# A small-batch gated feed-forward with gathered LoRA weights on one core: section three's weights queued after A of tile 1, both A gathered ahead of both B, splits reordered

## The reference

```python
def lora_add(base, inp, A, B):            # A: (16, 16, ·), B: (16, ·, 16)
    Ab, Bb = A[0][lora_indices], B[0][lora_indices]      # one adapter per sequence
    t = einsum('bri,bni->bnr', Ab, inp)
    return base + einsum('bor,bnr->bno', Bb, t) * 0.5
gate = lora_add(x @ W_gate.T, x, A_gate, B_gate)         # F = 1376 columns
up   = lora_add(x @ W_up.T,   x, A_up,   B_up)
x = x + lora_add((silu(gate) * up) @ W_down.T, silu(gate) * up, A_down, B_down)
x = x + einsum('bct,bcd->bdt', x, weights[condition])    # a 32x32 mix per sequence
```

## Time and profile before

| | |
|---|---|
| median of 3 runs | 449.8 us (449.45 to 450.18) |
| the profiled execution | 449.22 us, of which the span is 447.4 us |
| PE busy | 439.1 us (98% of the span) |
| DVE, ACT, POOL busy | 335.8 (75%), 212.5 (47%), 170.3 us (38%) |
| moved by DMA | 81.12 MB, mean 181 GB/s |

### The profile page before, as it was taken

The page is one execution under the profiler, slowest core; times in us unless marked ns, Lnnn a source line. Parts: engine busy times, 40 slices in busy tenths (PEclk is TensorE's granted clock), DMA queues, the critical chain, the costliest instruction groups (busy, mean ns, idle before and its releaser), DMA issues.

```text
span 447.4 us, 7255 instructions
## 1 busy us (share of the span) xinstructions
PE 439.1 (98%) x2477; PEld 394.7 (88%) x2477; DVE 335.8 (75%) x625; ACT 212.5 (47%) x397; POOL 170.3 (38%) x156
## 2 busy tenths in 40 slices
PE   7989999999999999999999999999999999999997
PEld 5868888888888888888888888999999999999996
DVE  6858989888866867867857858977767766776665
ACT  6736345456444444444543444844444454444541
POOL 2711322130111221121121452675666766666630
PEclk9989999999999999999999999999999999999999
DMA  8965664448476565565565599847667666656631
GB/s 240 379 209 159 167 174 134 111 163 199 120 197 158 146 180 149 159 172 146 158 171 145 144 283 347 241 136 194 210 186 209 208 197 179 175 174 191 195 100 47
DMA packets 99987, 81.12 MB, mean 181 GB/s; under 512 B 50960, under 2 KB 83344, under 8 KB 99952
## 3 DMA queue, kind: packets, MB, share of 16 engines
q1 hardware_dynamic: 88512, 47.15, 37.9%
q0 software_dynamic: 11008, 33.30, 24.8%
q10 hardware_dynamic: 432, 0.22, 0.2%
HBM read 65.18 MB, written 15.47 MB: 180 GB/s over the span
## 4 chain that ended last, share of the span: by engine, by line
PE 93%; DMA 2%; POOL 2%; issue 1%; DVE 1%; ACT 0%; SPq 0%; POOLq 0%
PE bank L1393 28%; PE bank L1271 9%; PE bank L1272 9%; PE bank L1270 9%; PE bank L1225 7%; PE bank L1226 7%; PE bank L1227 7%; PE bank L1292 5%; PE bank L1293 4%; PE bank L1423 2%; POOL a_raw L455 2%; PE bank L1403 2%; DMA a_raw<-in_a_gu_rows,rows 1%; DMA gu_landing<-in_w_gate 1%; PE bank L1408 1%
## 5 line engine op out<-in xcount | busy, mean ns | idle before, releaser
L455 POOL DMA_INDIRECT b_raw<-in_b_rows,rows x48 | 51.9, 1082 | 189.8 <-DVE b_gu L809 188.4
L1393 PE MATMUL bank<-wd,actT_hi 128*128 128x288 f32 (+1 forms) x636 | 110.1, 295 | 0.1
L1393 PEld LDWEIGHTS bank<-wd,actT_hi 128*128 128x128 f32 (+1 forms) x636 | 93.8, 188 | 2.1 <-issue 0.9
L455 POOL DMA_INDIRECT a_dn_raw<-in_a_dn_rows,rows x64 | 77.7, 1214 | 19.5 <-issue 19.5
L809 DVE SCALAR_TENSOR_TENSOR b_gu<-b_raw,low_rows,b_gu 128x1024 fp32r<-128x1024 f32 (+1 forms) x48 | 55.6, 1158 | 24.2 <-ACT b_gu L515 20.4
L1393 PE MATMUL bank<-wd,actT_lo 128*128 128x288 f32 (+1 forms) x318 | 68.2, 296 | 0.7 <-issue 0.7
L1393 PEld LDWEIGHTS bank<-wd,actT_lo 128*128 128x128 f32 (+1 forms) x318 | 51.0, 188 | 0.4 <-issue 0.4
L515 ACT ACTIVATE b_gu<-b_raw 128x1024 fp32r<-128x1024 f32 (+1 forms) x48 | 46.2, 963 | 9.6 <-DMA b_raw<-in_b_rows,rows 7.8
L605 ACT ACTIVATE act<-bank 128x512 f32<-128x512 f32 (+1 forms) x48 | 26.2, 547 | 44.0 <-PE bank L1293 43.9
L916 DVE TENSOR_TENSOR act<-act,bank 128x512 f32<-128x512 f32 (+1 forms) x48 | 29.9, 623 | 9.2 <-PE bank L1293 7.6
L1292 PE MATMUL bank<-b_gu,tT_hi 128*128 128x512 f32 (+1 forms) x96 | 35.6, 371 | 0.3 <-DVE tT_lo L805 0.3
(11 more groups left out here) (180 smaller groups left out, 1009.7 us busy)
## 6 DMA issues: line engine op xcount, KB each, us to landing
actT_raw<-actT_dram SPq DMA_DIRECT2D x16, 640.0 KB
actT_dram<-staging SPq DMA_DIRECT2D x64, 128.0 KB
x_sb<-in_x SPq DMA_DIRECT2D x16, 256.0 KB
xT_raw<-in_xT SPq DMA_DIRECT2D x15, 256.0 KB
out<-out_sb SPq DMA_DIRECT2D x15, 256.0 KB
a_raw<-in_a_gu_rows SPq DMA_DIRECT2D x56, 64.0 KB
actT_dram<-staging SPq DMA_DIRECT2D x32, 88.0 KB
wd_raw<-in_w_down SPq DMA_DIRECT2D x10, 256.0 KB, 5.8
```

The source lines that it names most:

```text
L455: return pool.indirect_dma_start(dst, None, src, bass.IndirectOffsetOnAxis(ap=rows[:, tile, col:col + 1], axis=0))
L1393: last = pe.matmul(ps_down[e][half][:, 0:HALF], a[e][0:n, c, :], wd[0:n, c, part, at:at + HALF], start=(c == 0 and i == 0), stop=(c == NC ...
```

## The change

The weights of section three (16 to 23) are queued by SP only when all four gathers of A of tile 1 have landed. POOL starts at another signal: x of tile 1 landed, instead of x of tile 0 split. It then gathers A of both tiles and after them B of both. ACT's and DVE's lists follow: A of tile 1 is split ahead of B of tile 0, and section three's pieces are split later, two of them between t of tile 0 and t of tile 1, two more behind the gating of unit 1 (on ACT behind its silu) instead of ahead of t.

```diff
--- before.py
+++ after.py
@@ -415,7 +415,9 @@
             sp.dma_start(xT_raw[0][:, 2 * P:KH * P], xT[0:P, 2 * P:KH * P]).then_inc(xT_landed[0], 16)
             load_gate_up(2, 2 * KH)
             load_xT(0, 1)
-            load_gate_up(2 * KH, GU_PIECES)
+            load_gate_up(2 * KH, 4 * KH)
+            sp.wait_ge(a_first_landed[1], 16 * TILE_SEQS)
+            load_gate_up(4 * KH, GU_PIECES)
             pair(0, first=True)
             pair(1)
             pair(2)
@@ -490,10 +492,10 @@
                 gather(mix_raw[m % 2][:, :], mix_rows, m, 2 * TILE_SEQS + 2).then_inc(mix_landed[m % 2], 16)
 
             pool.wait_ge(rows_ready, 1)
-            pool.wait_ge(xT_ready[0], 1)
+            pool.wait_ge(xT_landed[1], 16)
             gather_first_a(0)
+            gather_first_a(1)
             gather_b(0, 0, 0)
-            gather_first_a(1)
             gather_b(0, 0, 1)
             for pr in range(PAIRS):
                 pair(pr)
@@ -687,17 +689,16 @@
             split_x(0, 1)
             split_weights(2 * KH, 4 * KH)
             split_a(0, 0)
-            split_weights(4 * KH, 4 * KH + 2)
+            split_a(0, 1)
             split_b(0, 0, 0)
-            split_weights(4 * KH + 2, 5 * KH)
-            split_a(0, 1)
             split_t(0, 0)
             split_b(0, 0, 1)
+            split_weights(4 * KH, 4 * KH + 2)
+            split_t(0, 1)
             silu(0, 0)
             split_b(0, 1, 0)
-            split_t(0, 1)
             silu(0, 1)
-            split_weights(5 * KH, 6 * KH)
+            split_weights(4 * KH + 2, 6 * KH)
             split_b(0, 1, 1)
             split_a(1, 0)
             silu(0, 2)
@@ -1052,19 +1053,19 @@
             split_x(0, 1)
             split_weights(2 * KH, 4 * KH)
             split_a(0, 0)
-            split_weights(4 * KH, 4 * KH + 2)
+            split_a(0, 1)
             ve.wait_ge(low_landed, 16)
             split_b(0, 0, 0)
-            split_weights(4 * KH + 2, 5 * KH)
-            split_a(0, 1)
             mask_t(0, 0)
             split_t(0, 0)
+            split_b(0, 0, 1)
+            split_weights(4 * KH, 4 * KH + 2)
             mask_t(0, 1)
-            split_b(0, 0, 1)
             split_t(0, 1)
             gate(0, 0)
             split_b(0, 1, 0)
             gate(0, 1)
+            split_weights(4 * KH + 2, 5 * KH)
             turn(0, 0)
             turn(0, 1)
             split_weights(5 * KH, 6 * KH)
```

## The result

| | before | changed |
|---|---|---|
| median | 449.8 us (449.45 to 450.45, 5 runs) | 452.63 us (451.84 to 453.83, 5 runs) |
| ratio | | 1.0072, 95% interval 1.0049 to 1.0096 |
| profiled execution, span | 449.22, 447.4 us | 453.83, 452.0 us |

The account below looks back on a forecast made before the run. PE was taken as the bound, with no slack after unit 4's start. L + 10.85 gives 36.75; plus 0.6 for the next gather, less the old 35.78, 1.57 us later: 449.8 + 1.6 = 451.4 us, range 449.6 to 453.3.

Parts of the forecast that it names:

- POOL's start and order: POOL's first gather at 11.3 us instead of 8.05; B of tile 0, ninth instead of fifth, starts at 22.0.
- Landing of A: Last gather of A of tile 1 lands at 23.9 us, `t_alone(1)` starts without a stall: 1.6 us gained on PE.
- L: Landing of B of section one for tile 0: 25.9 us, against 20.27 before; bounds 24.1 to 28.3.
- From L to unit 4: Chain of splits, masks and `lora(0,2)` from L to the start of unit 4: 10.85 us, so 36.75.
- The next gather: B of section two for tile 0, gathered once B of section one is split: 5.9 us to land, adding 0.6.
- rival (b): Clock falls again after PE's waits before `lora(0,0)` and `lora(0,2)`; if unit 4 runs low too, 453.1 us; chance 0.15.
- The rule of the Trainium skill: DMA engines alternate between queues with work, so the 0.6 us for B of section two would fall away: 450.8.
- Rival (a): The gathers run fast and the kernel is faster or the same, 449.0 us at L = 24.1; chance 0.23.
- Hidden parts: Two splits moved behind unit 1's gating cost nothing, cover 0.1 us; SP's loads of A of pair 1 end by 39.8.

Follow-up runs that it names:

- the control: The changed kernel once more, without an edit, beside the kernel before on the same chip: 453.24 us, where the kernel before had 449.58.
- the controls: The kernel before and the changed kernel, each run once more without an edit: 449.83 and 453.24 us.

## Why the prediction was right, and where it was off

Direction and range held, the range narrowly for the control (453.24 of 453.3); the size was too small by 1.2 us (1.6 forecast, 2.8 measured, 3.4 between the controls). The mechanism was the forecast one; one term of its sum, the next gather, was far too small.

- **POOL's start and order**: 11.3 forecast, 11.40 measured; B of section one starts at 22.0 and 22.40. Right.
- **Landing of A**: 23.9 and 23.5; no wait ahead of `t_alone(1)`. Right: the goal of the change was reached, 1.6 us of stall removed. The 64 KB gather took 2.4 us on quiet DMA (21.15 to 23.5), less than my 3.1.
- **L**: 25.9 and 26.1. Right. `lora(0,0)`: 29.75 and 29.94, PE idle 3.1 us.
- **From L to unit 4**: 10.85 forecast. In the four profiles in which ACT doesn't wait for B of section two it was 11.1 (three times) and 11.4. Right within 0.5.
- **The next gather**: here the sum failed. I took 5.9 us for B of section two and 0.6 us for its lateness. Beside the held weights it took 7.2, 7.1, 6.9, 7.6 and 7.5 us (five profiles); behind weights that wait for it 4.3 to 4.5 (three). Unit 4 then starts 3.5 us after its landing, 4.1 to 4.3 if the clock is low. In the changed kernel's profile that makes 2.4 us instead of 0.6 (0.7 of it is the low clock in `lora(0,2)`, see rival (b)), in its control 1.7. The 5.9 came from the gather at 45.52, of which the prediction says that DMA was full. The share was 0.98 and 0.89, but little was moved, against 392, 421 and 373 GB/s beside the gather in the changed kernel. In the kernel before:

```profile
46.00:48.00 2.00, 2.00 (x11) 1.65 (x10) 2.00 (x2) 0.03 (x1) 1.21 (x2) 1.00 0.98 168
48.00:50.00 2.00, 2.00 (x11) 1.71 (x10) 1.67 (x4) 1.09 (x2) 1.17 (x1) 1.00 0.89 301
```

- **The 4.64 us of the profile** add up: L + 11.1 is 37.2 instead of 35.78, 1.4 us; the next gather 2.4; unit 4 at the low clock 0.85.
- **The rule of the Trainium skill** ("DMA: Bandwidth & Descriptors", "Queues, rings and completion order") was taken to make this term nothing. The page says that each engine takes turns, not that a turn costs nothing: with an even share of the 367 GB/s of the earlier trace rows, an estimate, 512 KB would take 1.4 us more than the 4.3 to 4.5 without a backlog. The runs bear neither out: it took 2.8 us more beside the backlog. Nor does an even share fit the 7.6 us for 352 KB in the kernel with old start and no hold.
- **Rival (b)**, a second low clock, came true in the changed kernel's first profile and not in its control. By the mean clocks it isn't the usual case: 4 of the 11 executions of the changed kernel have 0.992, as much low clock as two spells of 3.6 us, and the other seven 0.995 or 0.996; the median execution, 452.63, has 0.995. It cost 0.7 us in `lora(0,2)` (37.91 to 39.57 instead of 0.95 us) and 0.85 in unit 4 (7.34 instead of 6.49), 1.6 for 3.4 us at the low level, against the 1.7 of the prediction; the Trainium skill's relation ("TensorE: Matmul & The Clock Gate", "Terms"), half the throttled time, agrees.
- **Rival (a)**, fast gathers, fell: POOL needed 11.0 us for eight, L was 26.1.
- **Hidden parts**: SP's loads of A of pair 1 ended at 38.4 and delayed nothing; the two splits moved behind unit 1's gating cost at most 0.1 us (unit 4 to unit 5 took 6.4 at full clock).

The cause in short: holding the weights until A of tile 1 has landed moves the backlog from that gather to the next one on the chain, B of section two. It is paid there, on top of B of section one that comes later by order and start. Undoing start or hold alone doesn't mend it (453.43, 453.67), undoing start and hold takes back part (451.83), keeping the weights clear of B of section two and the old start takes back all (449.97). What gather order and reordered splits cost is not told apart, for the splits were not tried by themselves. Together they may cost up to 3 us: the last figure was measured with them in place (ratio 1.0009), the kernel with four pieces held and the old lists has 0.9943.

## What to carry to other kernels

Transfers that are held back do not vanish, they meet whatever is in flight when they are released: look which gather runs then and who waits for it. Hold back only what is wanted last, release it when no gather of the chain is under way or when the one that is has time to spare, and leave the order of the others alone. With four pieces held, B of section two had started at 22.24, the up pieces came behind A of tile 2 at 25.69, and ACT wanted B only at 28.20: four pieces instead of eight, with the old lists, gave 0.57% where the whole change lost 0.72%. On an engine with a fixed list, a step placed behind one transfer also delays what only looks unrelated, here the masks of t behind B.

## What was not expected of the hardware

- The same place in the same kernel brought a low-clock spell of 3.4 us in one execution, behind a stall of 1.60 us, and of 6.8 in another, behind 2.59 (the first profile before and its control). A second stall of 2.11 us brought one where a stall of 1.45 did not, and with the weights not held a stall of 2.48 us brought none. The length of a stall alone doesn't tell whether the clock falls.
- The mean granted clock of an execution goes with its time: with POOL's old start from 450.2 us at 1.000 to 454.6 and more at 0.989.
- POOL takes 0.85 us from its first signal to its first gather, whichever signal it is (7.20 to 8.05 before, 10.55 to 11.40 after), and 0.27 for later ones; with DMA quiet its gathers come every 1.25 us.
- In the down projection, between 298 and 310 us, the same matmuls had 0.7 us of idling in some executions and lost 1 to 3.3 us more in others, with the clock at 0.68 and 0.69 from 305 to 310 us in two (weights not held, POOL's old order); no wait for another engine stands before them. How much of the spread from run to run comes from there is not shown, and its cause stays open.
